# A graph network's second gate: pairs of tiles staged differently, node rows added from 32-row products, query rows from 64-row quarters

## The reference

```python
def _gate(h, q, Wg, bg, Wq, bq):          # h: 64 x 768, q: 8 x 64 x 768
    B, L, F = q.shape
    N = h.shape[0] // B                   # 8 nodes in each batch
    h3 = h.reshape(B, N, F)
    hg = jnp.einsum('bnf,gf->bng', h3, Wg[:, :F])
    qg = jnp.einsum('blf,gf->blg', q, Wg[:, F:]) + bg
    attn = jax.nn.sigmoid(hg[:, :, None, :] + qg[:, None, :, :])
    qi = jnp.einsum('bnlf,blf->bnf', attn, q)
    alpha = jax.nn.sigmoid(h3 @ Wq[:, :F].T + qi @ Wq[:, F:].T + bq)
    return (alpha * jnp.tanh(qi) + (1.0 - alpha) * h3).reshape(B * N, F)
```

## Time and profile before

| | |
|---|---|
| median of 3 runs | 286.42 us (286.4 to 287.89) |
| profiled execution | 286.82 us |
| its span, first to last instruction | 284.9 us |
| TensorE busy | 263.1 us, 92% |
| VectorE busy | 145.5 us, 51% |
| ScalarE busy | 93.4 us, 33% |
| GpSimd busy | 93.6 us, 33% |
| mean granted TensorE clock | 0.986 |

### The profile page before, as it was taken

The page is one execution under the profiler, slowest core; times in us unless marked ns, Lnnn a source line. Parts: engine busy times, 40 slices in busy tenths (PEclk is TensorE's granted clock), DMA queues, the critical chain, the costliest instruction groups (busy, mean ns, idle before and its releaser), DMA issues.

```text
span 284.9 us, 3987 instructions
## 1 busy us (share of the span) xinstructions
PE 263.1 (92%) x1605; PEld 122.7 (43%) x1605; DVE 145.5 (51%) x252; ACT 93.4 (33%) x155; POOL 93.6 (33%) x80
## 2 busy tenths in 40 slices
PE   7999999999899989999996899999989979998994
PEld 7764854455345522344332223223434343433441
DVE  0835540019999998430148797983541135114512
ACT  2412420035759976020025656741200041003000
POOL 7480000004999998000035888950000000000000
PEclk9999999999999999999999999999999995999999
DMA  7999995992009856006999500000897090000001
GB/s 243 369 401 401 402 351 175 408 403 91 0 0 329 337 167 171 0 2 238 404 403 401 215 0 2 0 0 2 319 402 276 0 330 3 0 0 2 1 2 28
DMA packets 21028, 51.84 MB, mean 182 GB/s; under 512 B 4105, under 2 KB 4361, under 8 KB 21010
## 3 DMA queue, kind: packets, MB, share of 16 engines
q1 hardware_dynamic: 20400, 51.35, 48.7%
q10 hardware_dynamic: 610, 0.24, 0.4%
HBM read 51.39 MB, written 0.20 MB: 181 GB/s over the span
## 4 chain that ended last, share of the span: by engine, by line
PE 65%; DVE 16%; POOL 9%; issue 7%; ACT 2%; DVEq 0%; POOLq 0%; ACTq 0%
PE ps L913 26%; POOL prod L527 9%; PE ps L1204 6%; PE ps L990 6%; PE ps L887 4%; DVE prod L773 3%; PE ps L965 3%; DVE pre L787 3%; PE ps L1104 3%; PE ps L1078 3%; PE ps L1049 2%; PE ps L971 2%; DVE stack L759 2%; PE ps L1270 2%; PE ps L949 1%
## 5 line engine op out<-in xcount | busy, mean ns | idle before, releaser
L527 POOL TENSOR_TENSOR prod<-pre,qn 128x768 f32<-128x768 f32 x38 | 74.0, 1969 | 11.4 <-ACT pre L603 9.0
L787 DVE TENSOR_TENSOR pre<-ps,qg 128x768 f32<-128x768 f32 x49 | 45.6, 950 | 8.0 <-PE ps L1078 7.3
L603 ACT ACTIVATE pre<-pre 128x768 f32<-128x768 f32 x49 | 41.2, 847 | 18.8 <-DVE pre L787 17.9
L913 PE MATMUL ps<-W,nodeT 128*64 128x384 f32 x216 | 39.8, 504 | 0.0
L913 PE MATMUL ps<-W,prod 128*64 128x384 f32 x240 | 39.5, 487 | 0.0
L1078 PE MATMUL ps<-stack,bsel 96*128 96x384 bf16 x128 | 31.5, 329 | 5.2 <-DVE pre L787 2.8
L990 PE MATMUL ps<-W 128*128 128x384 f32 x96 | 34.7, 490 | 0.9 <-DVE W L389 0.7
L389 ACT COPY W<-ps 128x384 f32<-128x384 f32 x40 | 18.2, 482 | 40.1 <-PE ps L887 40.0
L1104 PE MATMUL ps<-prod,rsel 128*32 128x384 f32 x256 | 27.3, 497 | 3.1 <-POOL prod L527 2.2
L517 POOL COPY stack<-hi 32x384 bf16<-32x384 bf16 x4 | 2.2, 555 | 78.3 <-DVE hi L751 78.1
L913 PEld LDWEIGHTS ps<-W,prod 128*64 128x64 f32 x240 | 16.6, 137 | 21.1 <-issue 20.2
(11 more groups left out here) (174 smaller groups left out, 230.2 us busy)
## 6 DMA issues: line engine op xcount, KB each, us to landing
W<-in_L_gnn_W SPq DMA_DIRECT2D x9, 2304.0 KB, 10.4
W<-in_L_gnn_W_rel SPq DMA_DIRECT2D x6, 2304.0 KB, 16.2
W<-in_L_gnn_Wg SPq DMA_DIRECT2D x4, 1152.0 KB, 11.9
W<-in_L_gnn_W_root SPq DMA_DIRECT2D x2, 2304.0 KB, 9.8
W<-in_L_gnn_Wq SPq DMA_DIRECT2D x4, 1152.0 KB, 8.0
qn<-in_L_gnn_query_embs SPq DMA_DIRECT2D x4, 384.0 KB, 11.1
xa<-in_x ACTq DMA_DIRECT2D x2, 96.0 KB, 7.5
out<-t SPq DMA_DIRECT2D x2, 96.0 KB, 2.2
```

The costliest lines, as they stand in the source:

```text
L527: nc.gpsimd.tensor_tensor(prod[:, T % PRODS, :], pre_of(T), qn[:, pair_and_node(t)[0], :], ALU.mult).then_inc(prod_p, 1)
L603: nc.scalar.activation(dst, src, ACT.Sigmoid).then_inc(sig_ready, 1)
L787: nc.vector.tensor_tensor(dst, ring(T), by_half(qg[:, pair_and_node(t)[0], :]), ALU.add).then_inc(pre_ready, 1)
L913: ins = nc.tensor.matmul(ps[c * N:(c + 1) * N, bank, 0:HD], T[:, j, col0 + h * N:col0 + (h + 1) * N], w[:, k, c * HD:(c + 1) * HD], start= ...
```

## The change

The second gate gets its own order, in pairs. Left tile k is T = 32 + 2k, right tile k is T = 33 + 2k, k from 0 to 15.

- Kinds: every right tile is P but the last, which is D. Left tiles are D or X: two D, then one X. T is gone.
- The three bf16 parts are no longer stacked. `low` is a tile of its own beside `hi` and `mid`. The selector `bsel` is built for four groups of 32 rows instead of three, and the node rows of a tile come from six products over 32 rows, for a left and a right tile together twelve.
- Left tiles of D, from the second step on, and the last right tile get their queries by four products over 64 rows and 64 output partitions. For the two quarters that cross over, `qs` holds the swapped halves of `qg`. Two DMAs make it, which SP issues behind `hg_done`. `qs` lies in the slot of L2_W2_0, whose load moves behind the second alpha. L2_W1_1 and L2_W1_2 stand behind the DMAs in SP's order.
- Left tiles use PSUM slots 0 and 1 in turn, right tiles slot 2 (the last one slot 0).
- The left tile k + 1 gets its nodes in the same step as right tile k.
- PRODS and `wait_prod_free` are as before. The first gate keeps its order, written out as `first_gate`.

```diff
-        bsel = sb("bsel", [3 * GN, PPG * NB, P], BF16)
-        i3 = sb("i3", [3 * GN, GN], BF16)
+        bsel = sb("bsel", [P, PPG * NB, P], BF16)
+        i4 = sb("i4", [P, GN], BF16)
+        i3 = i4[0:3 * GN, :]
...
+        low = sb("low", [P, HD], BF16)
...
+        qs = W[SLOT["L2_W2_0"]][:, 0:2, :].rearrange("p a (b f) -> p (a b) f", b=2)
...
-            return t % 2 if T < TILES or t % 2 == 0 else 1 + t // 2 % 2
+            if T < TILES:
+                return t % 2
+            return t // 2 % 2 if t % 2 == 0 else 0 if t == TILES - 1 else 2
...
-            "TD" "PX" "PX" "PP" "PD" "PX" "PX" "PP" "PX" "PD" "PX" "PP" "PX" "PD" "PX" "XD")
-        AHEAD = (TILES, TILES + 1)
+            "DP" "DP" "XP" "DP" "DP" "XP" "DP" "DP" "XP" "DP" "DP" "XP" "DP" "DP" "XP" "DD")
+        AHEAD = (TILES, TILES + 2)
...
+        SIGMOIDS = list(range(TILES)) + [left(0)] + [
+            T for k in range(HALF_T - 1) for T in (left(k + 1), right(k))] + [right(HALF_T - 1)]
...
             load("L2_W1_0", a["L2_gnn_W1"][0], rgcn_done, done + 2)
+            sp.wait_ge(hg_done, 2)
+            for c in range(2):
+                sp.dma_start(qs[c * N:(c + 1) * N, :, :],
+                             qg[(1 - c) * N:(2 - c) * N, :, c * HD:(c + 1) * HD]).then_inc(qs_loaded, 16)
             load("L2_W1_1", a["L2_gnn_W1"][1], rgcn_done, done + 3)
             load("L2_W1_2", a["L2_gnn_W1"][2], rgcn_done, done + 4)
-            load("L2_W2_0", a["L2_gnn_W2"][0], hg_done, 2)
-            load("L2_W2_1", a["L2_gnn_W2"][1], alpha_done, 2)
+            load("L2_W2_0", a["L2_gnn_W2"][0], alpha_done, 2)
+            load("L2_W2_1", a["L2_gnn_W2"][1])
...
+                    nc.vector.tensor_tensor(low[:, :], t1[:, :], mid[:, :], ALU.subtract).then_inc(low_ready, 1)
...
+                    add(right(0))
+                    multiply(left(0))
+                    for k in range(1, HALF_T):
+                        multiply(left(k))
+                        if k + 1 < HALF_T and KINDS[left(k + 1)] == "X":
+                            add(left(k + 1))
+                        if KINDS[right(k)] == "P":
+                            add(right(k))
+                    multiply(right(HALF_T - 1))
...
+            def copy_queries_by_rows(T):
+                p = pair_and_node(T % TILES)[0]
+                for c in range(2):
+                    rows = slice(c * N, (c + 1) * N)
+                    nc.tensor.matmul(ring(T)[rows, c, :], ident[rows, rows], qg[rows, p, c * HD:(c + 1) * HD],
+                                     start=True, stop=False)
+                for c in range(2):
+                    rows = slice(c * N, (c + 1) * N)
+                    other = slice((1 - c) * N, (2 - c) * N)
+                    nc.tensor.matmul(ring(T)[other, c, :], ident[rows, rows], qs[rows, p, :], start=True, stop=False)
+
+            def add_nodes_rows(tiles):
+                for part in (hi, mid, low):
+                    for T in tiles:
+                        t = T % TILES
+                        for c in range(2):
+                            rows = slice(c * N + t % 2 * GN, c * N + (t % 2 + 1) * GN)
+                            ins = nc.tensor.matmul(ring(T)[:, c, :], bsel[rows, t // 2, :], part[rows, :],
+                                                   start=(part is hi and KINDS[T] != "D"), stop=(part is low))
+                        if part is low:
+                            ins.then_inc(hg_cast, 1)
...
+            def second_gate():
+                LAG = 2
+                ALPHA_AT = {5: 0, 7: 1, 8: 2, 10: 3, 11: 4, 13: 5}
+                pe.wait_ge(hi_ready, 2)
+                pe.wait_ge(mid_ready, 2)
+                pe.wait_ge(low_ready, 1)
+                add_nodes_rows((left(0), right(0)))
+                add_nodes_rows((left(1),))
+                keep_warm(5, TRB)
+                for k in range(1, HALF_T + LAG):
+                    if k == 2:
+                        pe.wait_ge(qs_loaded, 32)
+                    tiles = ()
+                    if k + 1 < HALF_T:
+                        wait_multiplied(pe, left(k - 1))
+                        if KINDS[left(k + 1)] == "D":
+                            copy_queries_by_rows(left(k + 1))
+                        tiles = (left(k + 1), right(k))
+                    elif k == HALF_T - 1:
+                        wait_multiplied(pe, left(k - 1))
+                        copy_queries_by_rows(right(k))
+                        tiles = (right(k),)
+                    if k + 1 < HALF_T:
+                        wait_added(pe, right(k - 1))
+                    if tiles:
+                        add_nodes_rows(tiles)
+                    if k < 4:
+                        keep_warm(3, TRB)
+                    if k in ALPHA_AT:
+                        if ALPHA_AT[k] == 0:
+                            add_bias("L0_gnn_bq", TRB)
+                        project(nodeT, WqT_h, TRB, first=False, last=False, chunks=[ALPHA_AT[k]])
+                    if k >= HALF_T:
+                        wait_added(pe, right(HALF_T - 2))
+                        keep_warm(2, 4)
+                    if k >= LAG:
+                        reduce_pair(left(k - LAG), k == LAG, k == HALF_T + LAG - 1)
```

More of the change, by code:

```diff
@@ L774, in multiply, with add @@
                                             by_half(qn[:, pair_and_node(T % TILES)[0], :]), ALU.mult).then_inc(prod_v, 1)
[L776 to L790, removed]
+                def add(T):
+                    wait_cast(dve, T)
+                    if KINDS[T] != "X":
+                        wait_pre_free(dve, T)
+                    dst = ring(T) if KINDS[T] == "X" else by_half(pre_of(T))
+                    nc.vector.tensor_tensor(dst, ring(T), by_half(qg[:, pair_and_node(T % TILES)[0], :]),
+                                            ALU.add).then_inc(pre_ready, 1)
+                if layer == 0:
+                    for t in range(TILES + LAG):
+                        if t % (TILES // 2) == 0 and t < TILES:
+                            wait_units_out(dve, UNITS // 2 * (1 + t // (TILES // 2)))
+                        if t < TILES:
+                            add(t)
+                        if t >= LAG:
+                            multiply(t - LAG)
+                else:
+                    add(right(0))
[7 more added lines that the diff above has]
+                    multiply(right(HALF_T - 1))
                 dve.wait_ge(reduced, (layer + 1) * TILES // 2)
@@ L1045, in _, with copy_queries @@
             query_unit(4, HALF2)
[L1047 to L1054, removed]
+            def copy_queries(T):
+                for c in range(2):
+                    nc.tensor.matmul(ring(T)[:, c, :], ident[:, :], qg[:, pair_and_node(T % TILES)[0], c * HD:(c + 1) * HD],
+                                     start=True, stop=False)
@@ new lines, in reduce_pair @@
+            def reduce_pair(T, first, last):
+                k = T % TILES // 2
+                s = GN - 1 - k // NB * 2 * NB - k % NB
+                for g in range(2):
+                    wait_multiplied(pe, T + g)
+                for c in range(2):
+                    for g in range(2):
+                        at = c * N + g * GN
+                        ins = nc.tensor.matmul(ps[at:at + GN, ACC, 0:HD], rsel[:, s:s + GN],
+                                               prod[:, (T + g) % PRODS, c * HD:(c + 1) * HD],
+                                               start=first, stop=last, skip_group_check=True)
+                ins.then_inc(reduced, 1)
@@ L1064, in gate @@
                     if TILES <= t < TILES + LAG - 1:
-                        keep_warm(1, TRA if layer == 0 else 2 * ring_slot(2 * TILES - 3))
+                        keep_warm(1, TRA)
                     if t < TILES:
[L1067 to L1074, removed]
+                        if t >= 2:
+                            wait_added(pe, t - 2)
@@ L1075, in gate @@
                         for c in range(2):
[L1076 to L1079, removed]
+                            ins = nc.tensor.matmul(ring(t)[:, c, :], bsel[0:3 * GN, t // 2, :],
+                                                   stack[:, c, t % 2, :], start=True, stop=True)
@@ L1080, in gate @@
                         ins.then_inc(hg_cast, 1)
[L1081 to L1085, removed]
+                        if t in UNIT_AT:
+                            query_unit(UNIT_AT[t][0], [UNIT_AT[t][1]])
                         if t == LATE_AT[0]:
@@ L1134, in _ @@
                     for T in AHEAD:
-                        for c in range(2):
-                            copy_queries(T, c)
+                        copy_queries(T)
                 if layer == 0:
@@ L1139, in _ @@
                     query_unit(SPLIT_UNIT)
-                gate(layer)
+                (first_gate, second_gate)[layer]()
                 keep_warm(1, 2)
```

103 lines of the change are left out of this document (54 added, 49 removed).

## The result

| | median, us | runs |
|---|---|---|
| before | 286.41 | 4 (286.3 to 287.89) |
| changed | 315.59 | 4 (312.87 to 318.82) |

Ratio 1.097, 95% interval 1.090 to 1.104. That is 29.2 us more where I had forecast 19.2. The profiled execution of the changed kernel is the slowest of its four (318.82, span 317.0), with a mean clock of 0.929 against 0.943 to 0.960 in the others, so what its trace shows of the clock is somewhat more than usual.

What follows compares the result with a forecast made beforehand. The second gate's loop of add, node products, multiply, add was taken as the bound. Turns of 3.41 us, X adds, alphas, warm-ups and tail end the gate at 213.0, not 193.8: +19.2, so 305.6 us; range 301 to 318.

Steps and rivals of the forecast that it cites:

- The wait that decides: Second gate: multiply of left k waits for the reduction of pair k-2, putting that reduction, hidden before, onto the path.
- the turn: Second gate, end of one right add to the next: 3.41 us, where the present loop takes about 2.65.
- Row groups four at once: Second gate's twelve node products run as three rounds of four: 0.48 us taken, 1.92 in single file.
- Rival 2: Row products not four at once: 312.3 in twos, 326 singly, 315.1 if weight loads go in single file; 14%.
- The start: Second gate's opening: one low cast of 0.65 us replaces four stack writes; add right 1 ends at 154.0.
- rival 3: TensorE's clock falls to half in the second gate: 0.48 + 0.65 us more a turn, 313.6 in total; 14%.
- the ring: Second gate's closed loop: right add, node products, reduction, left multiply, next right add; alpha and warm-ups lengthen it.
- Rival 1: Second gate: the work saved counts, 2.2 us a D pair, three pairs in 6.6, gate end 190, total 282.5; 6%.
- The DMAs: Two swap transfers of query halves, 2.0 us at 395 GB/s, land about 151, before step 2 needs them at 153.1.

Runs made afterwards that it cites:

- e3: Changed kernel with TensorE's waits in the second gate filled by products nobody reads, orders and waits unchanged: 308.65 us, ratio 1.078 to the kernel before.
- e1: Changed kernel with eight product buffers in the second gate instead of four: 282.78 us, ratio 0.991 to the kernel before.
- e2: Changed kernel, four buffers, with the reduction of pair k-2 at the head of TensorE's step instead of its end: 291.89 us, ratio 1.022 to the kernel before.
- e6: Changed kernel with six product buffers in the second gate instead of four: 284.09 us, ratio 0.993 to the kernel before.
- e4: The kernel before, in its old order, with eight product buffers and L2_W2_0 loaded behind the second alpha: 287.47 us, ratio 1.001.
- e5: e1 with whole 128-row query copies in place of the ten sets of four 64-row quarters: 290.76 us, ratio 1.015 to the kernel before.
- e7: Changed kernel with eight buffers, no warm-ups in steps 1 to 3, alpha moved to steps where TensorE waits: 281.6 us, ratio 0.981 to the kernel before.
- e9: e7 with six more warm-up products ahead of the attention weights of the first RGAT layer: 279.64 us, ratio 0.973 to the kernel before.
- e8: Changed kernel, four buffers, with alpha products and warm-ups behind their step's reduction instead of ahead of it: 301.3 us, ratio 1.045 to the kernel before.

## Why the prediction was right, and where it was short

**The wait that decides: right.** The sum put the turn at 3.41 us. At full clock, from the right add that ends at 153.68 to the one that ends at 157.90, it is 4.22 with the warm-ups: 0.05 + 0.60 + 0.75 + 0.85 + 0.14 + 0.88 + 0.95. Without the warm-ups 3.47. The two small misses are the hand-over to VectorE (0.14 between the timeline's rows, 0.09 taken from the chain) and three warm-ups at 0.75 for 0.68, the change of shape included. Over the gate they make 13 x 0.06 + 2 x 0.07 = 0.9 us; e3, at full clock, ends it 1.3 us later than forecast. e1, e2 and e6 open this wait by buffers or by order, and the kernel is 24 to 33 us shorter, the clock's part included.

**Row groups four at once: right.** This was the open cost, 0.48 to 1.92. Node products of the changed kernel's second step, weight loads and products:

```profile
153.73 0.34 PE L1117 MATMUL ps<-hi,bsel 32*128 32x384 bf16 x4 [0.37 <-DVE pre L815]
153.74 0.10 PEld L1117 LDWEIGHTS ps<-mid,bsel 32*128 32x128 bf16 x4
153.91 0.33 PE L1117 MATMUL ps<-mid,bsel 32*128 32x384 bf16 x4
153.91 0.10 PEld L1117 LDWEIGHTS ps<-low,bsel 32*128 32x128 bf16 x4
154.07 0.33 PE L1117 MATMUL ps<-low,bsel 32*128 32x384 bf16 x4
```

Three rounds 0.16 to 0.18 apart, and four weight loads within 0.10 us. What the Trainium skill says of weight loads ("TensorE: Matmul & The Clock Gate", Step-by-step: what each phase is for), time by columns and not by rows, agrees with the trace for a single load: 0.10 us with 32 rows, 0.097 with 96. But the four of a round lie beside each other, and the rounds follow each other no slower for them. Rival 2 is out, its 315.1 too. That the result, 315.59, lies beside that 315.1 is chance.

**The start: right, by other terms.** Add right 1 was to end at 154.0 and ends at 153.68. Low and mid together take 0.92 where I had 0.71 + 0.65: without the stack copies beside it the mid cast takes 0.36 instead of 0.71. The nodes then wait for TensorE's own query copies ahead, which end at 148.6, and not for VectorE. That the other engines' copies slowed the cast is argued from these two traces; no run separates it.

**The clock: mis-sized.** This is where most of the missing 10 us lie. The forecast put nothing for rival 3 into its sum and gave it 14%. It came, on top of the ring. In the profiled executions the gate is 13.7 us longer than in e3, where the clock stays full (228.0 against 214.3). My price, 0.48 + 0.65 a turn, is what a half-clock turn shows (1.15 for 0.67 and 1.48 for 0.83, and 0.68 more where alpha stands in it); the weight wasn't right. I took the us of 0.33 busy in the earlier trace rows as a sign that the clock bears idle time. It was a single one, and e4 shows the clock falling behind that very wait. In the changed kernel each turn had more than 1 us of idle time. Turns with only that ran at 1.00 for a while (170 to 175 us, TensorE busy for 3.05 of 5), and the two waits of 2.1 us before 162.26 and 176.30 stand right ahead of half-clock windows. In the profiles, the ring and the clock are not independent: before, e1, e2, e5, e6, e7 and e9 hold 1.00 through the gate without fillers, and long half-clock stretches stand only in the changed kernel. Two kernels show a single one of some 3.5 us: e8, which has the ring, and e4, which hasn't.

**What is left.** The medians give 6.9 us between the changed kernel and e3, but that is not all that the clock costs in the gate, since e3 has the late dip. An estimate: at full clock the span of the profiled execution would be 317.0 - 13.7 = 303.3; the spans of the other three, 311.1, 313.2 and 314.4, are 8 to 11 us above that, the median of the four 10.5. The kernel before has its late dip in its profile; beside the experiments it took 284.0 to 284.5 in the executions with a mean clock of 0.997 or more, some 2 us less than its median. So 29.2 is 19.2 forecast + 1.3 for the gate at full clock (0.9 of it the links above) + about 10.5 for the clock in the gate - about 2 for the late dip, 29.0. Only the profiled executions show where the clock was low, so this split of the medians stays an estimate.

**Rival 1's price was too low, and its total came out by luck.** Two D steps of its 2.2 us are 4.4, not the 3.9 that it adds. With the X step of 2.7 three pairs take 7.1 us, where it has 6.6. In e7, where alpha is covered, they take 7.02 (X adds at 172.57 and 179.60), in e1 7.82 with two alphas. So e1's gate ends at 191.8 and not 190; its total of 282.78 lies beside the rival's 282.5 because six of its ten executions (282.5 to 282.9, mean clock 0.997 or more) lack the late dip, which the 286.42 that the rival counts from has.

**The DMAs: right that they don't matter, the rate was off.** The swap transfers land 4.4 us after their issue at 145.85 and 146.6 (the page and the timeline), so by about 151, ahead of the first use at 152.49. The windows from 148 to 152 us show 234 and 253 GB/s instead of 395; the weight load issued at 147.3 shares in them.

## To carry along

When two engines' orders are written by hand, follow the loop of every buffer, not only of the one that the change is about: a reduction that was hidden becomes the bound if the wait that frees its buffer stands behind the work that its own result releases. A change that saves work on every engine came out 29 us slower for want of one pair of buffers. With that pair it is 0.7% faster than the kernel before (e6), and with the side work moved and the late wait filled 2.7% (e9). Of its parts only the quarters were measured by themselves (e5). Put side work (alpha, warm-ups) behind the instruction that another engine waits for; in e8 that shortened the ring by 6.2 us and left one short stretch of low clock in the gate.

## What I had not expected of the hardware

A cast of 128x384 from fp32 to bf16 on VectorE took 0.71 us while GpSimd and ScalarE copied, and 0.36 in the changed kernel, where they did not. Weight loads of four row groups ran within 0.10 us. Behind a wait of 1.45 us in a late stage the clock was low for about 7 us in some profiles (before, e7) and not in another (e1); six more warm-up products of 0.22 us removed that and 2 us of the scatter. The same waits at 152 to 154 us left the clock full in one profile (before) and were followed by 3.5 us at half clock in another (e4).
